# Fourth attention layer: the mask of two score groups added by four 64x64 identity matmuls in the quarters of the array

## The reference

```python
Q = split(q @ Wq.T + bq); K = split(k @ Wk.T + bk); V = split(v @ Wv.T + bv)
scores = einsum('bhqd,bhkd->bhqk', Q, K) / sqrt(8)
scores = where(mask == 0, -1e9, scores)          # mask 1x1x256x1601, integers
attn = softmax(scores, axis=-1)
out = einsum('bhqk,bhkd->bhqd', attn, V)          # heads joined, then @ Wo.T + bo
```

## Time and the profile before

| | |
|---|---|
| time, median of 3 runs | 2402.89 us (2401.49 to 2403.20) |
| the profiled execution's own time | 2405.89 us |
| its span, from the first to the last instruction | 2404.1 us |
| mean granted clock of TensorE | 0.911 |
| the changed stage in it | from about 1958 to 2363 us |

### The profile page before, as it was taken

The page is one execution under the profiler, slowest core; times in us unless marked ns, Lnnn a source line. Parts: engine busy times, 40 slices in busy tenths (PEclk is TensorE's granted clock), DMA queues, the critical chain, the costliest instruction groups (busy, mean ns, idle before and its releaser), DMA issues. The chain is left out here.

```text
span 2404.1 us, 44599 instructions
## 1 busy us (share of the span) xinstructions
PE 2066.4 (86%) x17629; PEld 1438.3 (60%) x17629; DVE 1358.7 (57%) x3398; ACT 1327.5 (55%) x2088; POOL 100.6 (4%) x335
## 2 busy tenths in 40 slices
PE   5499999945844799799999999999994559999997
PEld 3377777723632467577777777777772326666663
DVE  4588888865442521555555545545545556666662
ACT  3499999931312733355555555555552326676763
POOL 1000000000011200000000000000000310000000
PEclk9699999976875989899999999999996669999997
DMA  6411111103232011000000000000000631111110
GB/s 216 168 58 53 53 56 54 46 14 114 80 102 89 4 36 35 36 1 1 1 1 1 1 1 1 2 1 1 1 1 10 228 117 60 52 59 54 58 37 13
DMA packets 50709, 115.32 MB, mean 48 GB/s; under 512 B 6476, under 2 KB 26732, under 8 KB 50508
## 3 DMA queue, kind: packets, MB, share of 16 engines
q1 hardware_dynamic: 44172, 82.25, 11.0%
q0 software_dynamic: 6336, 30.28, 3.6%
HBM read 81.71 MB, written 30.80 MB: 47 GB/s over the span
## 5 line engine op out<-in xcount | busy, mean ns | idle before, releaser
L2316 ACT ACTIVATE a_prT<-bank 128x512 f32<-128x512 f32 (+1 forms) x448 | 232.7, 565 | 328.0 <-PE bank L2225 327.8
L1488 DVE CUSTOM_DVE_ANT_0 a_attn_junk<-wide,a_mask 128x801 f32<-128x801 f32 (+1 forms) x256 | 247.0, 992 | 125.5 <-PE wide L1319 124.1
L1431 ACT ACTIVATE a_attn_prT<-bank 128x512 f32<-128x512 f32 (+1 forms) x448 | 237.2, 566 | 119.7 <-PE bank L1336 98.3
L2341 DVE CUSTOM_DVE_ANT_0 a_sc<-wide,a_zeros 128x1024 f32<-128x1024 f32 (+1 forms) x256 | 243.1, 988 | 91.8 <-PE wide L2211 91.8
L1777 DVE CUSTOM_DVE_ANT_0 a_attn_sc<-wide,a_mask 128x801 f32<-128x801 f32 (+1 forms) x256 | 252.9, 989 | 18.4 <-PE wide L1631 16.2
L1647 PE MATMUL bank<-ident,a_attn_sc 128*128 128x128 f32 x1664 | 244.9, 276 | 15.3 <-ACT a_attn_prT L1736 14.1
L1647 PEld LDWEIGHTS bank<-ident,a_attn_sc 128*128 128x128 f32 x1664 | 198.8, 141 | 62.6 <-issue 42.7
L2225 PE MATMUL bank<-ident,a_sc 128*128 128x128 f32 x1664 | 231.2, 277 | 1.5 <-ACT a_prT L2316 1.5
L2225 PEld LDWEIGHTS bank<-ident,a_sc 128*128 128x128 f32 x1664 | 185.4, 141 | 54.4 <-issue 28.1
L1742 ACT ACTIVATE a_attn_sc<-a_attn_sc,a_attn_nmx 128x1601 f32<-128x1601 f32 x128 | 209.6, 1638 | 8.5 <-DVE a_attn_nmx L1783 8.5
L2211 PE MATMUL wide<-a_kT,a_qT 64*128 64x512 f32 (+1 forms) x1024 | 211.0, 529 | 0.0
(11 more groups left out here) (432 smaller groups left out, 2800.7 us busy)
## 6 DMA issues: line engine op xcount, KB each, us to landing
a_ks<-a_k_parts SPq DMA_DIRECT2D x128, 225.1 KB
a_proj_ctxb<-in_ctxT SPq DMA_DIRECT2D x12, 832.0 KB, 5.1
a_k_parts<-a_proj_kp POOLq DMA_DIRECT2D x24, 416.0 KB, 5.7
a_v_rows<-a_proj_vb POOLq DMA_DIRECT2D x8, 936.0 KB, 8.4
a_vs<-a_v_rows SPq DMA_DIRECT2D x32, 234.0 KB
a_q_stack<-a_proj_qp POOLq DMA_DIRECT2D x18, 256.0 KB, 4.4
a_qx<-a_q_stack SPq DMA_DIRECT2D x128, 36.0 KB
ctxT<-in_ctxT SPq DMA_DIRECT2D x4, 832.0 KB, 12.7
```

The source lines that it names most:

```text
L1431: act.activation(prT[0:keys, u % PRT, kt:kt + m, :], bank_of(s, f"W{g}")[0:keys, 0:m * S].rearrange("p (t q) -> p t q", q=S), ACT.Exp).the ...
L1488: dve.tensor_tensor_reduce(junk[:, n % 2, 0:w], S_WIDE[n % 2][:, 0:w], mask(qt, at, w), 1.0, LOWEST, ALU.add, ALU.max, mx[:, p % 2, qt, e, ...
L2316: copy = lambda out, src: act.activation(out, src, ACT.Copy)
L2341: dve.tensor_tensor_reduce(sc[:, s % 2, h, at:at + w], S_WIDE[h][:, 0:w], zeros[:, 0:w], 1.0, LOWEST, ALU.add, ALU.max, mx[:, s % 2, h, p: ...
```

## The change

The masks of two groups (W0 and W1, W2 and W3, W4 and W5) are added together, by four matmuls with a 64x64 piece of the identity as the weight, each in its own quarter of the array: the even group's mask lies on partitions 0 to 63 and goes through the upper half of the rows, the odd group's on 64 to 127 and through the lower half; `side` 0 fills partitions 0 to 63 of a bank and `side` 1 the others. Each of the four has 512 columns, both key tiles at once. The score matmuls stay as they are and follow the four. W6 is alone: two mask matmuls of 256 columns, with weights of 64 and of 1 column. The waits for both banks stand ahead of the four. `score_piece` and the other items take their places between the pairs. The mask tensor has a new layout of 4 x 2 x 512 columns, brought into form on the host.

```diff
-            def turned_group(s, g):
+            def turned_pair(s, first):
                 u = s - TURN
                 if not 0 <= u < UNITS:
                     return
-                if g == 0 and u % 2 == 0:
+                pair = [g for g in (first, first + 1) if g < NG]
+                if first == 0 and u % 2 == 0:
                     pe.wait_ge(rows_in, u // 2 + 1)
-                bank_free(s, f"W{g}")
-                bank = bank_of(s, f"W{g}")
-                kt, m = GROUPS[g]
-                for j in range(m):
-                    at, keys = (kt + j) * P, min(P, SC - (kt + j) * P)
-                    out = bank[0:keys, j * S:(j + 1) * S]
-                    pe.matmul(out, core.identb[:, 0:keys], maskT(kt + j), start=True, stop=False)
-                    ins = pe.matmul(out, ks[:, u % RING, at:at + keys], qx[:, u % RING, :], start=False, stop=True)
-                ins.then_inc(turned, 1)
+                for g in pair:
+                    bank_free(s, f"W{g}")
+                for side in range(2):
+                    for g in pair:
+                        kt, m = GROUPS[g]
+                        r = g % 2
+                        keys = min(HALF, SC - kt * P - side * HALF)
+                        pe.matmul(bank_of(s, f"W{g}")[side * HALF:side * HALF + keys, 0:m * S],
+                                  core.identb[r * HALF:(r + 1) * HALF, r * HALF:r * HALF + keys],
+                                  maskT[r * HALF:(r + 1) * HALF, g // 2, side, 0:m * S], start=True, stop=False)
+                for g in pair:
+                    kt, m = GROUPS[g]
+                    for j in range(m):
+                        at, keys = (kt + j) * P, min(P, SC - (kt + j) * P)
+                        ins = pe.matmul(bank_of(s, f"W{g}")[0:keys, j * S:(j + 1) * S], ks[:, u % RING, at:at + keys],
+                                        qx[:, u % RING, :], start=False, stop=j == m - 1)
+                    ins.then_inc(turned, 1)
...
             for s in range(LAST):
                 values(s)
-                turned_group(s, 0)
+                turned_pair(s, 0)
                 score_piece(s, 0)
-                turned_group(s, 1)
-                turned_group(s, 2)
+                turned_pair(s, 2)
                 score_piece(s, 1)
                 mix(s)
-                turned_group(s, 3)
                 rows(s)
                 turn_u(s)
-                turned_group(s, 4)
+                turned_pair(s, 4)
                 score_piece(s, 2)
-                turned_group(s, 5)
                 output(s)
                 score_piece(s, 3)
-                turned_group(s, 6)
+                turned_pair(s, 6)
...
-            mask, maskT = sb("a3_mask", [P, 2, SC]), sb("a3_maskT", [P, KT, S], BF16)
+            mask, maskT = sb("a3_mask", [P, 2, SC]), sb("a3_maskT", [P, 4, 2, 2 * S], BF16)
...
-                seenT = core.sb(inner, "a3_seenT", [P, KT, S], I32)
+                seenT = core.sb(inner, "a3_seenT", [P, 4, 2, 2 * S], I32)
...
-                    (seenT[:, :, :], inp["mask3T"].rearrange("(t p) q -> p t q", p=P))])
+                    (seenT[:, :, :, :], inp["mask3T"])])
```

More of the change, by code:

```diff
@@ L1230, in quad_attention_stage @@
     GROUPS = [(kt, min(2, KT - kt)) for kt in range(0, KT, 2)]
-    NG = len(GROUPS)
+    NG, HALF = len(GROUPS), P // 2
     CHUNKS = [(0, 7), (7, KT)]
@@ L1827, in masked_head_layer @@
     v_rows = nc.dram_tensor(name + "_v_rows", (B, P, HEADS, KT * VCOLS), F32, kind="Internal").ap()
-    STACK, RING, V_RING = 72, 6 if maskT else 4, 3
+    STACK, RING, V_RING = 72, 6 if maskT is not None else 4, 3
     half = (SC + 1) // 2
@@ L1837, in clear @@
         def clear(pool, sem):
-            if not maskT:
+            if maskT is None:
                 return
@@ L1858, in load_values @@
             sp.dma_start(vs[:, k, :, :], v_rows[b, :, h:h + 4, :]).then_inc(sem, 16)
-        if maskT:
+        if maskT is not None:
             quad_attention_stage(core, name + "_attn", acc, wot, load, load_values, ks, qx, vs, mask, maskT)
@@ L2481, in _ @@
                                           ALU.mult).then_inc(scaled3, 1)
-                        dve.tensor_scalar(maskT[:, :, :], seenT[:, :, :], 0.0, MASKED, ALU.is_equal,
+                        dve.tensor_scalar(maskT[:, :, :, :], seenT[:, :, :, :], 0.0, MASKED, ALU.is_equal,
                                           ALU.mult).then_inc(scaled3, 1)
                         dve.wait_ge(scaled3, 2)
-            masked_head_layer(core, "a3", core.x, lambda qt, at, n: mask[:, qt, at:at + n], lambda kt: maskT[:, kt, :],
+            masked_head_layer(core, "a3", core.x, lambda qt, at, n: mask[:, qt, at:at + n], maskT,
                               w, cols, cols[:, 2:3], wot[:, :], bo[:, :])
@@ L2506, in lay_out @@
     a["mask3"] = g["mask_1x1xSxS2_ik0"].reshape(S, SC)
-    a["mask3T"] = np.ones((SCP, S), g["mask_1x1xSxS2_ik0"].dtype)
-    a["mask3T"][:SC] = a["mask3"].T
+    seen = np.ones((8 * 2 * P, S), g["mask_1x1xSxS2_ik0"].dtype)
+    seen[:SC] = a["mask3"].T
+    a["mask3T"] = seen.reshape(4, 2, 2, 2, P // 2, S).transpose(1, 4, 0, 3, 2, 5).reshape(P, 4, 2, 2 * S)
     a["rank"] = np.arange(EXPERTS, 0, -1).astype(np.float32)
```

## The result

The changed kernel took 2480.82 us (median; 2478.44 to 2482.44), beside 2402.45 us for the kernel before on the same chip (2401.49 to 2403.2). The ratio is 1.0326 with a 95% interval of 1.0308 to 1.0344. The prediction said 2477 us, range 2446 to 2520.

A forecast was written before the change was run, and what follows sets the result against it. TensorE (PE) bounds the kernel before; two-bank waits add a hand-off chain. Steps 69.1, last units 2.1, batch ends 0.9, mask tensor 1.8: 73.9 us on 2405.9 gives 2479.8, median 3.0 lower: 2477, range 2446 to 2520.

The forecast's parts named there:

- The four quarters run at once: Pair's mask block: four 64x64 tiles start within some 0.02; block 0.34 us, way in 0.09, so 0.43 for 0.44.
- Rival 2: Quarters run two and two, not four at once: each pair block 0.21 us longer, 40 more, 2517 us; 14%.
- The one-column tile switches: Last group's mask block: the one-column weight gets a narrower tile and one more switch; block 0.40 us, low end 0.21.
- Rival 1: Last group's one-column tile needs no switch: 0.18 to 0.19 us less per unit, 12 less, 2465 us; 22%.
- The hand-offs: Pair to pair through block, score, exponential, release: 1.59 us a unit's first, 1.51 its second, 2.01 with the rows item.
- Rival 4: Hand-off to ScalarE doesn't bind, PE's own work decides: 0.20 to 0.35 us more per step, 2416 to 2430; 7%.
- The release of 0.14: PE restarts 0.14 us after the exponential where a pair has two waits; bound 0.05, which takes 12 us off.
- Rival 3: The double wait ahead of a pair costs no more than a single one: 2465 us; 6%.
- Streamed columns (2365): Rival: TensorE alone bounds the stage; a pair block costs its stream, 0.23 us for 0.44, so 2365 us; 4%.
- Steps: Four-unit cycle: first (rows, copy of u) +1.13 us, second (plain) +1.06, third (rows) +1.17, fourth (values) +0.96; together 4.32, 16 times.
- Last three steps: Last three units, no score pieces left: chain gives 5.11 us for 3.34, +1.77 instead of mean 1.08; 2.1 in all.
- Batch ends: At three batch ends mix and output enter the ring: 0.3 us each, estimated as half an exponential; 0.9 in all.

The follow-up runs named there:

- experiment 5: Changed kernel with each exponential cut to 64 columns of one key tile, other probabilities a constant 0.5: 2447.31 us, ratio 1.02.
- 6: Kernel before with the exponentials cut to 64 columns of one key tile, other probabilities a constant 0.5: 2409.40 us, ratio 1.0039.
- experiment 1: Changed kernel, but the last group W6 gets its mask by one full 128x65 matmul again: 2463.56 us, ratio 1.0267.
- experiment 3: Kernel before with its full 128x128 mask matmuls, but in the pairs' order with both waits ahead of each pair: 2442.15 us, ratio 1.0174.
- experiment 2: Changed kernel, but PE waits only for the later bank of a pair where exponentials free both: 2473.14 us, ratio 1.0298.
- experiment 4: Kernel before, own order and waits, but each two-tile group's mask added by two 128x64 column halves of 512 columns: 2485.38 us, ratio 1.0364.
- experiment 11: The changed kernel run again, unchanged: 2483.07 us, ratio 1.0328.
- 7: Changed kernel with W6's mask by one full matmul and one wait per pair where exponentials free both banks: 2448.82 us, ratio 1.0209.
- 10: Changed kernel with W6's full mask matmul, single waits where exponentials free both banks, and mix ahead of the second pair: 2447.06 us, ratio 1.0187.
- 8: Kernel before, but the rows item uses a zero-filled 128-column weight, so it has no switch of form: 2397.25 us, ratio 0.9992.
- 9: Changed kernel, but at batch ends the item mix stands ahead of the pair W2 and W3, not behind it: 2479.57 us, ratio 1.0323.

## Why the prediction was right

**The four quarters run at once: right.** Starts within 0.01, score matmul 0.34 after the first mask, as worked out. Rival 2 (2517) is out. The block with its way in costs what the four full matmuls cost; with the chain taken away (experiments 5 and 6) all that is left is 1.56 in four units, of which the last group's switches are 1.2 to 1.3, so the three pairs indeed come out nearly even, at some 0.02 a block.

**The one-column tile switches: right.** 0.22 apart, block 0.42 for 0.40. Rival 1 (2465) is out. Experiment 1 gives its price as 1.29 per four units, where I had 1.22.

**The hand-offs: right to 0.01.** 1.59 and 1.51 in the plain step. With the rows item between, 2.00, for 2.01:

```profile
2137.33 0.41 PE L1337 MATMUL bank<-a_maskT,identb 64*64 64x512 bf16 x4 [0.30 <-ACT a_attn_prT L1437]
...
2139.33 0.41 PE L1337 MATMUL bank<-a_maskT,identb 64*64 64x512 bf16 x4 [0.50 <-ACT a_attn_prT L1437]
```

Rival 4 (2416 to 2430) is out by the 37.2 us of idle time and by experiment 3. Its sum for TensorE alone was sound: experiments 5 and 6 give 1.56. Its "0.20 to 0.35 more" per step was not: by the prediction's own terms the plain second step comes to 3x0.79+4x0.35+0.40+0.12+4x0.09 = 4.65 for 4.23, 0.42 more, and experiments 5 and 6 show 0.48 there, 0.34 to 0.38 in the others.

**The release of 0.14: right,** and its bound of 0.05 too, which experiment 2 has where one wait is left. Rival 3 is out.

**Streamed columns (2365): wrong.** The block is 0.34 and its way in some 0.1, for a stream and starts of 0.23. Experiment 4 streams as many columns in time as the kernel before and is 3.6% slower. The Trainium skill (TensorE: Matmul & The Clock Gate, Measured speedup vs the span model) counts some 4 ns per further tile; inside the block the trace agrees (0.01 for three further starts), but the 0.1 on each side of it isn't in that figure.

**Steps: 4.32 predicted, 4.48 measured,** so 71.7 us and not 69.1. The third step looks off most (1.28 for 1.17) and the first too long (1.10 for 1.13), but that is where I booked a switch: the 0.09 of the way into the next step's first pair stood with the step that it ends, while the distances of last groups count it in the step that begins. Moved, the forecasts are 1.06, 1.26, 0.96 and 1.04, and each step is short by 0.02 to 0.06. The plain step shows 0.03 to 0.04 of that: the last group's block is 0.42 and not 0.40, and from its score matmul to the next pair it is 0.22 to 0.23 (2130.18 to 2130.41) and not 0.21.

**Last three steps:** 5.11 predicted, 5.11 measured for the last two.

**Batch ends: the term that failed.** I put 0.3 on each by half an exponential; it was 1.3 (the two steps around each grew by 1.50 and 1.24 over the steady ones, where they grew by 0.66 and 0.79 before). PE in the step of such an end and right after it:

```profile
2099.24 0.41 PE L1337 MATMUL bank<-a_maskT,identb 64*64 64x512 bf16 x4
...
2101.33 0.41 PE L1337 MATMUL bank<-a_maskT,identb 64*64 64x512 bf16 x4 [0.79 <-ACT a_attn_prT L1437]
...
2103.41 0.41 PE L1337 MATMUL bank<-a_maskT,identb 64*64 64x512 bf16 x4 [0.56 <-ACT a_attn_outT L1461]
...
2105.85 0.30 PE L1344 MATMUL bank<-a_qx,a_ks 128*65 128x256 bf16 x1
2107.33 0.41 PE L1337 MATMUL bank<-a_maskT,identb 64*64 64x512 bf16 x4 [1.18 <-DVE x L1526]
```

Two waits make up the 1.3. In the step itself mix takes a slot of the ring: (W2, W3) now waits for the exponential of W1 and (W4, W5) for mix's own copy, so the pairs start 2.09 and 2.08 apart and not 1.59 and 1.51. With the matmuls of both items the step grew by 1.50 where it grew by 0.66 before: 0.84 more. After it, the output item has taken the bank that W1 gets next, and VectorE's addition frees it late. Before, only W1 waited for that (0.62 us); now W0 stands in the same pair and waits too, and ScalarE has nothing for that long: 0.45 more (1.24 for 0.79). It is the change's own mechanism, two banks for one start, at a place where I hadn't followed it. Three times 1.0 are 3 us.

**Mask tensor:** conversion 2.29 for 1.89, 0.4 as predicted:

```profile
1877.52 2.29 DVE L2488 TENSOR_SCALAR a_maskT<-a_seenT 128x4096 bf16<-128x4096 int32 x1
```

Its transfer was put at 1.4 and cost 0.3. The DMA issues after (KB, us from issue to landing), for the earlier trace rows:

```profile
a_seenT<-in_mask3T SPq DMA_DIRECT2D x1, 2048.0 KB, 12.5
a_seen<-in_mask SPq DMA_DIRECT2D x1, 1601.0 KB, 8.2
```

A quarter more bytes landed in nearly the same time. The old layout moves 1 KB at a stretch, the new one 16 KB per partition; that this is why was not tried.

**The closeness of the numbers** is partly luck. The layer grew by 79.4 us (0.7, 1.2 and 77.5), where the sum has 73.9. In the two profiles that hardly shows (72.6), only because the stretches outside the layer, which the change doesn't touch, came out 6.8 shorter (2.9 ahead, 3.9 behind). The medians don't have this help: they differ by 78.4, and 2477 for 2480.8 is short by 4 us. Even there errors cancel: steps, first cycle and batch ends were too low by some 7, the last steps and the mask's transfer too high by some 2.

Where the loss sits, then, by the runs, in four units: the order and its double waits 2.00 (experiment 3 over the kernel before); the quarters in the three pairs 1.19 (experiment 1 over experiment 3), nearly all of it the longer head of each pair, which lies on the chain (the pairs start 1.59 and 1.51 apart and in experiment 3 1.46 and 1.37); the last group's switches 1.29 (the changed kernel over experiment 1). Together 4.48. In whole times, on one chip, the first two are 42.6 and 21.4 us (with the two falls of the clock in experiment 1), and some 14 to 17 are left for the third.

## What to carry to other kernels

In this kernel array tiles would pay only for work long enough, or shared widely enough, to carry one switch in and one out: here 0.20 us per block against 0.21 saved. Before tying two buffers to one start, count the ring: with three buffers, a start that needs two of them leaves the consumer one to work on, and the loop then runs at the length of the hand-off (block, score, exponential, release), not at the busier engine's pace. Check every item that shares the ring (outputs, sums at a batch end) for the same wait, not only the steady step. A ring of four banks wasn't tried.

## What the hardware showed beyond that

**A switch costs nearly the same whatever the forms.** Full to column halves 0.08 (experiment 4), full to quarters 0.11 to 0.12 (0.22 to 0.23 after a score matmul of 0.11), full to a 6-column tile 0.09. The difference between halves and quarters isn't there behind a score piece: its last matmul is followed after 0.13 by a full one, and after 0.22 by halves (experiment 4) and by quarters (experiment 5) alike. Behind a block of 512 columns, halves or quarters, the full matmul starts 0.34 after the first. So the number of changes counts first. A weight of one column behaves as a form of its own, even beside a 64-column tile of the same rows: 0.22 apart, where tiles of one form start within 0.01. Other narrow widths weren't tried there. The Trainium skill (TensorEngine Tiling (Array Packing), Tiling Modes) says that changing the mode drains TensorE. The trace agrees: the full matmul starts 0.34 after tiles of 512 columns, where a full one of 512 columns is followed after 0.22.

**A fulfilled wait isn't free.** A second wait ahead of a matmul costs 0.09 after the first is released (0.14 against 0.05), though its own semaphore was reached long ago (experiment 2).

**The clock can fall in the middle of the busy stage.** After a batch end PE stands idle for 1.2 to 1.6 us in the kernels with pairs. In some executions the granted clock was then 0.50 (1.2 GHz) for a few us: in experiment 11's profile for 10.2 us from 2109.4, where the two steps took 9.11 and 10.41 instead of 7.07 and 8.47, 4.0 us in all. The windows above show PE 4.47 busy of 7.00 ahead of the fall, and 9.95 of 10.00 in it. The profile of experiment 2 has the same, once:

```profile
2102.00:2112.50 10.50, 10.41 (x65) 4.04 (x67) 3.91 (x8) 4.22 (x8) 0.16 (x1) 0.53 0.18 56
```

It came twice for 6.8 us in experiment 1, twice for 3.4 in each of 5 and 7, and once for 6.8 in 10; not at all in the first profile of the changed kernel, in the kernel before, or in experiments 3, 4, 6, 8 and 9. Nor does idle time of this length always do it: experiment 3 stands idle for 1.61 at all three batch ends, the changed kernel's first profile for 1.18, both at a clock of 1.00. So the fall isn't in the steps from which the loss was worked out, but it moves single executions of such kernels by up to 4.5 us (experiment 1), and how many of those that weren't profiled had one isn't known. That the idle time sets it off is suggested by the place, and wasn't tested by itself.
